# A planned attention and expert kernel: the negated maxima's transfers move from SyncE to ScalarE, with a new plan

## The chip, the cores and the metric

One core of a Trainium2 chip runs the kernel. The metric is the device time of one execution in microseconds, the median of several runs. PE is the tensor engine, DVE the vector engine, ACT the scalar engine (ScalarE), POOL GpSimd, SP the sync engine (SyncE), which here only issues transfers.

## What is computed

One pre-norm transformer layer in float32: causal attention with 16 heads of 16 columns, each row of the output scaled by a learned gate, then a mixture of experts (8 experts, 2 chosen for each token, and a shared one). B = 8 batches, S = 1024 tokens, E = 256 columns.

```python
Q, K, V = x @ Wq + bq, x @ Wk + bk, x @ Wv + bv        # x normalized, 16 heads
logits = jnp.einsum('bqhd,bkhd->bhqk', Q, K) * scale   # causal
attn = jax.nn.softmax(logits, axis=-1)
gate = jnp.tanh(g @ g_w2 + g_b2)[..., 0]               # g from a small network on x
x = x + einsum('bhqk,bkhd->bqhd', attn * gate, V) @ Wo + bo
...
h = silu(einsum('td,efd->tef', x, w1)) * einsum('td,efd->tef', x, w3)
x = x + einsum('tef,edf,te->td', h, w2, ew) + shared   # x normalized again
```

## The kernel before, in words

The work is cut into items: a kind of two letters and its place, as ("EX", n, g, s, p), batch n, group g of four heads, step s, pair p. `plan_work` lists all items with their engine, a cost in ns, a due time and the items that must come first; `Plan.run` then goes through a model of the five engines and picks for each engine, among the items that could start now, the one with the smallest due time. Two numbers bend this: `LATER` adds ns to the due time of a kind, and `SAME_TILING` is added to the due time of a PE item whose tiling of the array differs from the last one's, so the larger it is the longer PE stays with one tiling. What comes out is a fixed order for each engine; each engine's program is a walk through its order (`all_work`), with semaphore waits. An engine does its instructions strictly in that order.

Around the change, for each group and each half c of the 1024 queries:
- LD (SP, L969) loads stacked queries and keys to q_st and k_st. M (PE, L1912, and L1920 for the causal bars) makes the logits once with queries on the partitions, MR (DVE, L1548 and L1551) takes their row maxima to mx.
- MT (PE, L1932) turns the maxima, MN (ACT, L1344) writes them negated to rows_of (neg_max is a view of it), SM moves them: two transfers of 4 KB (L976) from rows_of to one row each of q_st, so that the scores come out with their maximum taken off.
- QK (PE, L1945) makes the scores with keys on the partitions. The first of each half waits for both transfers (semaphore nm_in). EX (ACT, L1362) takes the exponentials to probs, MK (POOL, L1179) masks the diagonal, PV (PE, L1965) sums them with the values, OE (ACT, L1371) copies the sums out and frees their bank.
- The tilings are rows for M and QK, columns for PV, full for everything else. Where the plan foresees that PE stands idle for 500 ns or more while sums are open, `keep_busy` puts up to eight filler matmuls there (L862), whose result adds zeros.

Beside these run the projections (L1882, L1896; DVE L1511 makes ql), the stores of queries and keys (SP L942, L943), the output projection (L1974), routing, and the experts (L2075, L2085, L2106; ACT L1423, L1438), with scatter and gather by POOL (L1211, L1223), the loads of routed rows xs<-xs_s (SP L1027) and, in the first batches, the clearing of their DRAM (SP L912, 512 KB each). SP issues every transfer but POOL's scatters and gathers, one after the other in its planned order. The plan charges SP ISSUE = 620 ns for each transfer.

Of the kernel before, what the change touches and what calls it, by code (L numbers as in the profile page):

```python
# [7 lines left out]
F32 = mybir.dt.float32  # L8
F32R = mybir.dt.float32r
ALU = mybir.AluOpType  # L10
ACT = mybir.ActivationFunctionType
# [9 lines left out]
PAIRS = GROUP // 2  # L21
# [3 lines left out]
GH = 16  # L25
# [14 lines left out]
QPC = CHUNK // P  # L40
# [59 lines left out]
ROWS_OF_HEAD = 64  # L100
# [8 lines left out]
FULL, ROWS, COLS = "full", "rows", "cols"  # L109
SWITCH, EXPOSED = 114, 104  # L110
PERIOD, KEEPS = 3413, 0.6
SAME_TILING = 14000
TAIL = {"PE": 155, "DVE": 88, "ACT": 112, "POOL": 45, "SP": 0}
HEARD = {"PE": {"PE": 0, "ACT": 37, "DVE": 37, "POOL": 75, "SP": 60}, "ACT": {"PE": 54, "ACT": 15, "DVE": 33, "POOL": 68, "SP": 60},
         "DVE": {"PE": 54, "ACT": 33, "DVE": 15, "POOL": 80, "SP": 60}, "POOL": {"PE": 54, "ACT": 33, "DVE": 33, "POOL": 40, "SP": 60},
# [1 line left out]
ISSUE = 620  # L117
# [60 lines left out]
def max_parts(u):  # L178
# [3 lines left out]
    for qt in qts:  # L182
# [4 lines left out]

LATER = {"AB": 8000, "AC": 15000, "AE": 22000, "AG": -1000, "AN": 4000, "AQ": -1000, "AR": -5000, "AS": -1000,  # L190
# [9 lines left out]


class Clock:
# [130 lines left out]
def plan_work():  # L333
    plan = Plan()
    add = plan.add
# [77 lines left out]
    def maxima(n, g):  # L413
        gi = n * GROUPS + g
        older = divmod(gi - 2, GROUPS)
        begin = at(n, g) - GROUP_T * 0.98
        for c in range(CHUNKS):
            m = g // (GROUPS // KE)
            add("SP", ("LD", n, g, c), 4 * ISSUE, begin - GROUP_T * (1.0 - 0.3 * c),
                [("PK", min(gi * CHUNKS + c + 1, K_HALVES - 1)), ("SQ", n, c, 2 * m), ("SQ", n, c, 2 * m + 1), ("QK",) + older + (LAST_STEP[c], SCORES[LAST_STEP[c]] - 1)],  # L420
                lands=9000 if n else 5000)
            units = [u for u in range(NMAX) if MAXU[u][0] == c]
            for u in units:
                _, p, kc, qts = MAXU[u]
                blocks = len(qts) * (1 if p is not None else PAIRS)
                due = begin + GROUP_T * 0.9 * u / NMAX
                add("PE", ("M", n, g, u), 240 if kc < c else 310 if blocks == 1 else 445, due,
                    [("BT",), ("LD", n, g, c), ("MT",) + older + (c,)], 2, ROWS)
                add("DVE", ("MR", n, g, u), sums(2 * sum(part[1] for part in max_parts(u)) * blocks // len(qts)) + 65 * len(qts), due + 1000, [("M", n, g, u)],
                    frees=(("M", n, g, u), None))  # L430
            due += 1500
            last = [("MR", n, g, units[-1])]
            if c:
                add("DVE", ("MJ", n, g), 95, due, last)
                last = [("MJ", n, g)]
            add("PE", ("MT", n, g, c), 60, due, last, 1, FULL)
            add("ACT", ("MN", n, g, c), 160, due, [("MT", n, g, c)] + ([("SM",) + divmod(gi - 1, GROUPS) + (c,)] if gi else []),
                frees=(("MT", n, g, c), None))
            add("SP", ("SM", n, g, c), 2 * ISSUE, due, [("MN", n, g, c)], lands=3600)

    def attention(n, g, s):
        c, kts, by_pair = STEPS[s]
# [192 lines left out]
def build(nc, ins, out):  # L635
# [4 lines left out]
    with ExitStack() as ctx:  # L640
# [161 lines left out]
        def q_half(n, g, c):  # L802
            return ((n * GROUPS + g) * CHUNKS + c) % Q_HALVES
# [79 lines left out]
        def _(sp):  # L883
# [84 lines left out]
                        to = q_st[r, q_half(n, g, c), :, :] if kind == 0 else k_st[r, k_half(n, g, c), :, :]  # L968
                        sp.dma_start(to.bitcast(F32), rows[j][:, :, cs]).then_inc(st_in[gi % 2][c], 16)  # L969

            def move_max(item, n, g, c):
                b, k = release["MN", n, g, c]
                sp.wait_ge(freed[b], k)
                for j in range(2):
                    to = q_st[ROWS_OF_HEAD * (j + 1) - 1:ROWS_OF_HEAD * (j + 1), q_half(n, g, c), :, :]
                    sp.dma_start(to.bitcast(F32), neg_max[j * PAIRS * QPC:(j + 1) * PAIRS * QPC, c, :].bitcast(F32)  # L976
                                 ).then_inc(nm_in[g % 2][c], 16)

            def store_o(item, n, g, c):
                b, k = release["OE", n, g, c]  # L980
                sp.wait_ge(freed[b], k)
# [70 lines left out]
            def load_ffn(item, i):  # L1052
                if i:
                    sp.wait_ge(wf_lo, i)
                sp.dma_start(wf_raw, ins["wf"][i]).then_inc(wf_in, 16)

            all_work(sp, "SP", {"AX": load_x, "WL": load_weights, "WC": load_constants, "BT": turn_bars, "XZ": clear_slots, "SQ": store_qk, "LD": load_stacks, "SM": move_max, "SO": store_o,
                                "CL": load_l, "CV": store_l, "CO": load_o, "SR": store_rest, "XL": load_slots,
                                "YS": store_slots, "RL": load_rest, "SY": store_y, "WF": load_ffn})
            for i in range(2):  # L1060
# [192 lines left out]
        def _(act):  # L1253
# [82 lines left out]
            def negate_max(item, n, g, c):  # L1336
# [3 lines left out]
                if gi:  # L1340
                    pn, pg = divmod(gi - 1, GROUPS)
                    if turn_of["QK", pn, pg, FIRST_STEP[c], 0] > turn_of["MT", n, g, c]:
                        act.wait_ge(nm_in[pg % 2][c], ((gi - 1) // 2 + 1) * 32)
                nc.scalar.activation(neg_max[:, c, :], bank(("MT", n, g, c))[0:GROUP * QPC, 0:P], ACT.Identity, scale=-1.0  # L1344
                                     ).then_inc(freed[release[item][0]], 1)

            def exponent(item, n, g, s, p):
                gs = (n * GROUPS + g) * NSTEP + s
                if first_wait("s_full", (n * GROUPS + g) * NSCORE + sum(SCORES[:s]) + p + 1):
                    act.wait_ge(s_full, (n * GROUPS + g) * NSCORE + sum(SCORES[:s]) + p + 1)  # L1350
                if p == 0 and gs >= 2:
                    of_group, older = divmod(gs - 2, NSTEP)
                    if turn_of["PV", of_group // GROUPS, of_group % GROUPS, older] > turn_of["QK", n, g, s, 0]:
                        if first_wait("pv_done", gs - 1):
                            act.wait_ge(pv_done, gs - 1)
                if SCORES[s] == PAIRS:
                    to, of = probs[:, s % 2, 2 * p:2 * p + 2, :], two_banks(("QK", n, g, s, p), CHUNK)
                else:
                    cols = CHUNK // PAIRS
                    to = probs[:, s % 2, :, 0:cols].rearrange("p (a j) c -> p j a c", j=2)  # L1360
                    of = two_banks(("QK", n, g, s, p), CHUNK).rearrange("p j (a c) -> p j a c", a=PAIRS)
                nc.scalar.activation(to, of, ACT.Exp, scale=DH ** -0.5).then_inc(freed[release[item][0]], 1)  # L1362
# [90 lines left out]
            def split_ffn(item, i):  # L1453
                if i == 0:
# [4 lines left out]
                nc.scalar.copy(hi, raw).then_inc(wf_hi, 1)  # L1459

            all_work(act, "ACT", {"AN": norm_x, "CM": mix_scale, "GC": gate_norm, "CN": norm_rest, "AC": copy_xt, "QH": queries_keys, "GE": gelu1, "GI": gelu2, "GL": gate_tanh,
                                  "MN": negate_max, "EX": exponent, "OE": copy_o, "CH": copy_hi, "XH": slots_hi,
                                  "CI": route_tanh, "RT": route_rows, "ET": expert_tanh, "HH": expert_high, "YC": copy_slots,
                                  "WH": split_ffn})

# [683 lines left out]
```

## Time and profile before

| | us |
|---|---|
| median of 3 runs | 1788.8 (1788.64 to 1791.04) |
| profiled execution, its time | 1798.91 |
| profiled execution, its span | 1797.1 |
| PE busy | 1650.4 (92%) |
| DVE, ACT, POOL busy | 1288.9, 1079.7, 810.5 |
| mean granted clock of PE | 0.968 |

Busy time is time in which an engine works on an instruction; issuing a transfer or waiting on a semaphore doesn't count. "SPq" is SP's queue issuing. "issue" in a chain or a wait is time in which nothing that the profile shows was waited for.

### The profile page before, as it was taken

Reading aid. Unit: us, or ns where it says so; the run is one execution under the profiler, and the core shown is the slowest. Engines: PE = TensorE matmul, PEld = TensorE weight load, DVE = VectorE, ACT = ScalarE, POOL = GpSimd, SP = SyncE. Lnnn points to the kernel's source line nnn. Section 1 sums busy time; section 2 is a strip of 40 time slices with the busy share of each in tenths; the row PEclk is TensorE's granted clock in tenths of the full one; section 3 lists DMA queues with packets and bytes.
Section 4 is the critical chain, followed back from the end, with each engine's and each line's share of the span. In section 5 each row is a group of like instructions: output and inputs, shape, how many; then the busy total and the mean of one; then the engine's idle time right before and its main releaser. Section 6 shows DMA issues by size and latency. Waiting matters only on the chain.

```text
span 1797.1 us, 34689 instructions
## 1 busy us (share of the span) xinstructions
PE 1650.4 (92%) x12770; PEld 979.4 (54%) x12770; DVE 1288.9 (72%) x2550; ACT 1079.7 (60%) x1808; POOL 810.5 (45%) x1390
## 2 busy tenths in 40 slices
PE   7799999889999999899998999999998989989889
PEld 3344455435544665456554566555654556657677
DVE  4777777857796768677696768877696656854666
ACT  3467755555657655675658666675557655657533
POOL 5325532453355221742238762543217674156761
PEclk9699999989999999999999999999999999999999
DMA  5557655544455444454455764534435655336440
GB/s 151 159 161 231 163 173 151 167 140 122 111 150 152 132 119 117 141 142 118 142 148 167 210 178 142 154 112 121 153 104 167 185 165 154 103 111 188 149 129 30
DMA packets 192709, 261.26 MB, mean 145 GB/s; under 512 B 19616, under 2 KB 127264, under 8 KB 192544
## 3 DMA queue, kind: packets, MB, share of 16 engines
q1 hardware_dynamic: 181792, 229.67, 44.3%
q0 software_dynamic: 10752, 29.37, 5.6%
q8 instruction: 105, 1.72, 0.4%
q14 instruction: 60, 0.49, 0.1%
HBM read 130.98 MB, written 127.40 MB: 144 GB/s over the span
## 4 chain that ended last, share of the span: by engine, by line
PE 53%; DVE 13%; ACT 10%; POOL 7%; DMA 7%; issue 5%; SPq 4%; another core or an unknown queue 1%; POOLq 0%; DVEq 0%; ACTq 0%
PE ps_all L2075 10%; PE ps_all L1965 10%; DVE mx L1551 6%; PE ps_all L1945 6%; PE ps_all L1912 6%; PE ps_all L2106 5%; ACT probs L1362 5%; PE ps_all L1896 4%; PE ps_all L1882 3%; PE ps_all L1974 2%; POOL xs_s L1211 2%; DMA qk_s<-ql 2%; PE ps_all L2085 1%; PE ps_all L1997 1%; DMA x<-in_x 1%
## 5 line engine op out<-in xcount | busy, mean ns | idle before, releaser
L1551 DVE TENSOR_REDUCE mx<-ps_all 128x2 f32<-128x1024 f32 (+2 forms) x640 | 620.6, 1005 | 157.1 <-PE ps_all L1912 84.2
L1362 ACT ACTIVATE probs<-ps_all 128x1024 f32<-128x1024 f32 x576 | 572.3, 1027 | 194.3 <-PE ps_all L1945 176.4
L1179 POOL TENSOR_SCALAR_AFFINE_SELECT probs<-probs 128x256 f32<-128x256 f32 (+1 forms) x448 | 190.8, 443 | 534.2 <-ACT probs L1362 529.9
L1965 PE MATMUL ps_all<-probs,vaug 128*32 128x512 f32 (+3 forms) x3072 | 323.0, 517 | 29.4 <-POOL probs L1179 18.9
L1912 PE MATMUL ps_all<-k_st,q_st 63*128 63x512 f32 (+3 forms) x1536 | 267.3, 399 | 41.0 <-ACT probs L1362 14.5
L1945 PE MATMUL ps_all<-q_st,k_st 64*128 64x512 f32 (+3 forms) x1536 | 262.3, 401 | 26.8 <-ACT probs L1362 11.8
L1912 PEld LDWEIGHTS ps_all<-k_st,q_st 63*128 63x128 f32 x1536 | 133.2, 190 | 162.7 <-issue 53.3
L1945 PEld LDWEIGHTS ps_all<-q_st,k_st 64*128 64x128 f32 x1536 | 128.9, 191 | 148.7 <-issue 65.6
L2075 PE MATMUL ps_all<-w_hi,x2h 128*128 128x512 f32 (+1 forms) x480 | 169.9, 354 | 3.2 <-DVE x2l L1600 2.2
L1808 DVE SCALAR_TENSOR_TENSOR act_t<-act_t,ps_all 128x256 f32<-128x256 f32 x168 | 70.2, 419 | 133.2 <-ACT act_t L1423 125.6
L1423 ACT ACTIVATE act_t<-ps_all 128x256 f32<-128x256 f32 x168 | 64.5, 385 | 161.3 <-PE ps_all L2075 116.4
L2075 PE MATMUL ps_all<-w_hi,x2l 128*128 128x512 f32 (+1 forms) x480 | 158.4, 330 | 0.0
L2075 PE MATMUL ps_all<-w_lo,x2h 128*128 128x512 f32 (+1 forms) x480 | 158.2, 330 | 0.0
L1965 PEld LDWEIGHTS ps_all<-probs,vaug 128*32 128x32 f32 x3072 | 72.3, 111 | 139.1 <-issue 96.9
L1211 POOL DMA_INDIRECT xs_s<-xnb,slot_u x112 | 111.9, 999 | 61.5 <-issue 41.3
L1223 POOL DMA_INDIRECT yab<-ys_s,slot_u x112 | 108.0, 964 | 33.0 <-issue 19.9
L2106 PE MATMUL ps_all<-w_hi,h_hi 128*128 128x256 f32 (+1 forms) x336 | 109.1, 325 | 4.8 <-DVE h_lo L1835 3.2
L2075 PEld LDWEIGHTS ps_all<-w_hi,x2h 128*128 128x128 f32 x480 | 92.4, 192 | 26.1 <-issue 17.6
L1438 ACT CAST h_hi<-ps_all 128x256 fp32r<-128x256 f32 x168 | 60.3, 374 | 63.9 <-PE ps_all L2085 57.0
L1882 PE MATMUL ps_all<-wvd,xt 128*128 128x384 f32 x256 | 96.3, 508 | 1.5 <-DVE ql L1511 0.9
L2075 PEld LDWEIGHTS ps_all<-w_hi,x2l 128*128 128x128 f32 x480 | 92.2, 192 | 8.6
L2075 PEld LDWEIGHTS ps_all<-w_lo,x2h 128*128 128x128 f32 x480 | 92.8, 193 | 5.6
(197 smaller groups left out, 2831.3 us busy)
## 6 DMA issues: line engine op xcount, KB each, us to landing
qk_s<-qh SPq DMA_DIRECT2D x116, 256.0 KB
q_st<-qk_s SPq DMA_DIRECT2D x128, 192.0 KB
k_st<-qk_s SPq DMA_DIRECT2D x128, 192.0 KB
xs<-xs_s SPq DMA_DIRECT2D x72, 256.0 KB
ys_s<-ysb SPq DMA_DIRECT2D x72, 256.0 KB
o_s<-o_sb SPq DMA_DIRECT2D x64, 256.0 KB
qk_s<-ql SPq DMA_DIRECT2D x57, 256.0 KB
xs_s<-ysb SPq DMA_DIRECT2D x20, 512.0 KB, 6.2
```

What stands on the lines that cost most here:

```text
L1179: last = nc.gpsimd.affine_select(out=block, in_=block, compare_op=ALU.is_ge, fill=0.0, base=0, pattern=[[0, heads], [1, P]], channel_multi ...
L1211: nc.gpsimd.indirect_dma_start(xs_s[i % 2], bass.IndirectOffsetOnAxis(ap=slot_u[:, n % 4, a, t:t + 1], axis=0), xnb[:, t, :], None).then_i ...
L1223: nc.gpsimd.indirect_dma_start(yab[:, t % 2, a, :], None, ys_s[SET_OF[n] % 2], bass.IndirectOffsetOnAxis(ap=slot_u[:, n % 4, a, t:t + 1], ...
L1362: nc.scalar.activation(to, of, ACT.Exp, scale=DH ** -0.5).then_inc(freed[release[item][0]], 1)
L1551: last = nc.vector.tensor_reduce(to[:, :, p, qt % QPC], both[:, :, at:at + keys], X_AXIS, ALU.max)
L1882: last = mm(bank(item)[:, 0:E + DP], xt[:, k, tt * P:(tt + 1) * P], wvd[:, k, :], start=(k == 0), stop=(k == KE - 1))
L1896: last = mm(bank(item), w[:, k, m * P:(m + 1) * P], xt[:, k, :], start=(k == 0), stop=(k == KE - 1))
L1912: last = mm(bank(item, j)[:, to:to + keys], q_st[r, q_half(n, g, c), p, qt % QPC * P:(qt % QPC + 1) * P], k_st[r, k_half(n, g, kc), p, 0:k ...
L1945: last = mm(bank(item, j)[:, to:to + cols], k_st[r, k_half(n, g, kt // QPC), a, kt % QPC * P:(kt % QPC + 1) * P], q_st[r, q_half(n, g, c), ...
L1965: last = mm(bank(first)[32 * h:32 * h + 32, q0 - c * CHUNK:], vaug[:, kt, g, h * VW:h * VW + 32], probs[:, s % 2, h, at:at + cols], start= ...
L2075: last = mm(bank(item)[:, to], x[:, buf, k, t * P:(t + 1) * P], w[:, k, cs], start=(k == 0 and j == 0), stop=(k == KE - 1 and j == 2))
L2106: last = mm(bank(first)[:, t * E:(t + 1) * E], h[:, z % 2, i * P:(i + 1) * P], w[:, cs], start=(item == first and i == 0 and j == 0), stop ...
```

## The change

SM becomes an item of ACT with a cost of 740 ns in the plan, and its two transfers are issued by ACT. `move_max` waits for the negation (which signals the semaphore of its bank) on ACT itself. SAME_TILING and the table LATER have other numbers.

```diff
-SAME_TILING = 14000
+SAME_TILING = 5000
...
-LATER = {"AB": 8000, "AC": 15000, "AE": 22000, "AG": -1000, "AN": 4000, "AQ": -1000, "AR": -5000, "AS": -1000,
...
+LATER = {"AB": 19000, "AC": 24000, "AE": 24000, "AG": 1000, "AN": 12000, "AQ": -1000, "AR": -15000, "AS": -9000,
...
-            add("SP", ("SM", n, g, c), 2 * ISSUE, due, [("MN", n, g, c)], lands=3600)
+            add("ACT", ("SM", n, g, c), 740, due, [("MN", n, g, c)], lands=3600)
...
-            def move_max(item, n, g, c):
-                b, k = release["MN", n, g, c]
-                sp.wait_ge(freed[b], k)
-                for j in range(2):
-                    to = q_st[ROWS_OF_HEAD * (j + 1) - 1:ROWS_OF_HEAD * (j + 1), q_half(n, g, c), :, :]
-                    sp.dma_start(to.bitcast(F32), neg_max[j * PAIRS * QPC:(j + 1) * PAIRS * QPC, c, :].bitcast(F32)
-                                 ).then_inc(nm_in[g % 2][c], 16)
...
+            def move_max(item, n, g, c):
+                b, k = release["MN", n, g, c]
+                act.wait_ge(freed[b], k)
+                for j in range(2):
+                    to = q_st[ROWS_OF_HEAD * (j + 1) - 1:ROWS_OF_HEAD * (j + 1), q_half(n, g, c), :, :]
+                    act.dma_start(to.bitcast(F32), neg_max[j * PAIRS * QPC:(j + 1) * PAIRS * QPC, c, :].bitcast(F32)
+                                  ).then_inc(nm_in[g % 2][c], 16)
```

In the changed kernel the lines up to the removed function stand 1 higher in number, those between it and the added one 7 lower, and those behind the added one 1 higher: the negation is L1337 there, the moved issues L1345, the exponentials L1363, the row matmuls L1913 and L1946, the sums L1966, the fillers L863.

SP's order near the start, batch 0, before (q_st<-rows_of is SM):

```order
L969 DMA q_st<-qk_s 48x2x512 x2
L969 DMA k_st<-qk_s 48x2x512 x2
L976 DMA q_st<-rows_of 1x8x128 x2
L969 DMA q_st<-qk_s 48x2x512 x2
L969 DMA k_st<-qk_s 48x2x512 x2
L942 DMA qk_s<-xs 8x16x512 x2
```

and ACT's order at the first maxima in the changed kernel (rows_of<-ps_all is the negation, probs<-ps_all an exponential):

```order
L1337 ACTIVATE rows_of<-ps_all 16x128
L1345 DMA q_st<-rows_of 1x8x128 x2
L1317 ACT_TABLE_LOAD
L1317 ACTIVATE vh<-vh 128x8x128
L1321 ACTIVATE gt<-gt 128x128
L1363 ACT_TABLE_LOAD
L1363 ACTIVATE probs<-ps_all 128x1024 x2
L1327 ACTIVATE gate<-drift,small 128x8
L1363 ACTIVATE probs<-ps_all 128x1024
L1337 ACTIVATE rows_of<-ps_all 16x128
L1345 DMA q_st<-rows_of 1x8x128 x2
```

SP's row L976 is gone from between the loads of stacks, and ACT has a row of two issues behind each of its 64 negations: directly behind it at 33, with other ACT work between at 31. Of the 33, 21 have an exponential or a copy of sums right behind them.

PE's order in batch 1, group 3, where the maxima of the next batch's first half are turned (L1932, then L1896 with wk), before:

```order
L1945 MATMUL ps_all<-q_st,k_st 128x512 x4
L862 MATMUL ps_all<-bars,scan 64x512 x3
L1932 MATMUL ps_all<-ident,mx 16x128
L862 MATMUL ps_all<-bars,scan 64x512 x8
L1896 MATMUL ps_all<-xt,wk 128x512 x2
L1965 MATMUL ps_all<-probs,vaug 32x256 x4
L1965 MATMUL ps_all<-probs,vaug 32x512 x4
L1945 MATMUL ps_all<-q_st,k_st 128x384 x2
```

and in the changed kernel:

```order
L1946 MATMUL ps_all<-q_st,k_st 128x512 x2
L1966 MATMUL ps_all<-probs,vaug 32x256 x4
L1946 MATMUL ps_all<-q_st,k_st 128x512 x2
L1946 MATMUL ps_all<-q_st,k_st 128x384 x2
L1946 MATMUL ps_all<-q_st,k_st 128x128 x2
L1946 MATMUL ps_all<-q_st,k_st 128x384 x2
L1946 MATMUL ps_all<-q_st,k_st 128x128 x2
L1933 MATMUL ps_all<-ident,mx 16x128
L1897 MATMUL ps_all<-xt,wk 128x512 x2
L1966 MATMUL ps_all<-probs,vaug 32x512 x4
L1946 MATMUL ps_all<-q_st,k_st 128x256 x4
```

The fillers around the turn are gone, four steps of scores stand ahead of it, and sums (L1966) come between scores, one row at a time. Over the whole order PE changes its tiling 1035 times before and 1132 times after, and has 120 fillers before and 71 after.

## Rows read from the trace of the kernel before

**Rows 1.** The page, its head, part 1 and the granted clock of part 2
```profile
span 1797.1 us, 34689 instructions
...
PE 1650.4 (92%) x12770; PEld 979.4 (54%) x12770; DVE 1288.9 (72%) x2550; ACT 1079.7 (60%) x1808; POOL 810.5 (45%) x1390
...
PEclk9699999989999999999999999999999999999999
```

**Rows 2.** The page, part 4, the chain that ended last, by engine
```profile
PE 53%; DVE 13%; ACT 10%; POOL 7%; DMA 7%; issue 5%; SPq 4%; another core or an unknown queue 1%; POOLq 0%; DVEq 0%; ACTq 0%
```

**Rows 3.** Windows: us, busy us of each engine, granted clock, DMA share, GB/s
```profile
0.00:300.00 300.00, 261.55 (x1911) 131.28 (x1912) 208.55 (x360) 175.12 (x262) 128.09 (x285) 0.93 0.60 172
...
600.00:900.00 300.00, 283.69 (x2255) 172.82 (x2251) 222.21 (x428) 181.57 (x305) 98.79 (x184) 0.99 0.46 129
```

**Rows 4.** The tile rows_of: durations min/median/max in ns
```profile
L976 SPq DMA_DIRECT2D q_st<-rows_of x128: 625/663/1994, 49.9 to 1611.5; - x128
L1344 ACT ACTIVATE rows_of<-ps_all x64: 247/262/269, 45.2 to 1610.5; 16x128 fp32r<-16x128 f32 x64
```

**Rows 5.** The chain in order of time, from 968 us: start, us, what
```profile
972.21 0.16 ACT rows_of L1344
972.37 0.02 issue
972.39 0.64 SPq L976
...
973.08 0.62 SPq L976
...
973.74 0.60 SPq L942
...
979.43 0.04 issue
979.47 6.83 DMA xs<-xs_s
```

**Rows 6.** Timeline of PE at 231.60: start, us, instruction, idle time before it
```profile
231.60 1.05 PE L1945 MATMUL ps_all<-q_st,k_st 64*128 64x512 f32 x4 [1.74 <-DMA q_st<-rows_of]
```

**Rows 7.** The chain in order of time, from 218 us
```profile
224.72 0.64 SPq L976
...
225.41 6.14 DMA q_st<-rows_of
...
231.60 1.05 PE ps_all L1945 x4
```

**Rows 8.** Who waited for whom, SP's queue: us in total, times, longest
```profile
SPq L976 <- ACT rows_of L1344: 72.6, 28, 8.4
```

**Rows 9.** Who waited for whom, all engines
```profile
POOL yab L1223 <- POOL rr L1236: 12.1, 36, 0.8
```

**Rows 10.** ACT's groups by line: busy, mean ns, idle before and its releasers
```profile
L1362 ACT ACTIVATE probs<-ps_all 128x1024 f32<-128x1024 f32 x576 | 572.3, 1027 | 194.3 <-PE ps_all L1945 176.4 <-issue 8.7 <-remote 6.5
```

**Rows 11.** Timeline of PE from 701 us, a change of tiling
```profile
701.08 0.28 PE L2106 MATMUL ps_all<-w_lo,h_hi 128*128 x1
...
701.20 0.28 PE L2106 MATMUL ps_all<-w_hi,h_lo 128*128 x1
...
701.41 0.50 PE L1912 MATMUL ps_all<-k_st,q_st 63*128 63x384 f32 x4
```

**Rows 12.** Timeline from 368 us: fillers, SP's long issues, PE's wait
```profile
370.26 1.91 PE L862 MATMUL ps_all<-bars,scan 128*64 128x512 bf16 x8
...
371.32 1.58 SPq L912 DMA_DIRECT2D xs_s<-ysb  x1
...
372.94 3.01 SPq L976 DMA_DIRECT2D q_st<-rows_of  x2
...
381.04 1.08 PE L1965 MATMUL ps_all<-probs,vaug 128*32 128x256 f32 x8 [6.96 <-POOL probs L1179]
...
385.86 3.37 PE L862 MATMUL ps_all<-bars,scan 128*64 128x512 bf16 x8
```

More of the change, by code:

```diff
@@ L1055, in load_ffn @@
                 sp.dma_start(wf_raw, ins["wf"][i]).then_inc(wf_in, 16)
-            all_work(sp, "SP", {"AX": load_x, "WL": load_weights, "WC": load_constants, "BT": turn_bars, "XZ": clear_slots, "SQ": store_qk, "LD": load_stacks, "SM": move_max, "SO": store_o,
+            all_work(sp, "SP", {"AX": load_x, "WL": load_weights, "WC": load_constants, "BT": turn_bars, "XZ": clear_slots, "SQ": store_qk, "LD": load_stacks, "SO": store_o,
                                 "CL": load_l, "CV": store_l, "CO": load_o, "SR": store_rest, "XL": load_slots,
@@ L1461, in _ @@
             all_work(act, "ACT", {"AN": norm_x, "CM": mix_scale, "GC": gate_norm, "CN": norm_rest, "AC": copy_xt, "QH": queries_keys, "GE": gelu1, "GI": gelu2, "GL": gate_tanh,
-                                  "MN": negate_max, "EX": exponent, "OE": copy_o, "CH": copy_hi, "XH": slots_hi,
+                                  "MN": negate_max, "SM": move_max, "EX": exponent, "OE": copy_o, "CH": copy_hi, "XH": slots_hi,
                                   "CI": route_tanh, "RT": route_rows, "ET": expert_tanh, "HH": expert_high, "YC": copy_slots,
```

19 rows, old and new, of the table LATER are left out of this document.

## The prediction

> **What bounds the kernel now.** I read the page's head first. The tensor engine is busy 92% of the span and holds 53% of the chain that ended last [rows 1, 2], so what changes the time is what makes PE wait or issue more. PE's idle time is 1797.1 − 1650.4 = 146.7 us, 8% of the span; ACT is busy 60% and holds 10% of the chain, DMA landings 7% and SP's own issuing 4%. The clock column and the windows say when PE ran slowly: 0.93 of full clock in the first 300 us, 0.99 from 600 to 900 [rows 1, 3].
>
> Then the transfers that the change moves. Each pair of SP issues at L976 follows one negation on ACT (L1344). The tile's view gives 128 issues of 663 ns in the median, 1994 ns at most, and 262 ns for a negation [rows 4]. In the chain SP starts 25 ns after the negation ends and is done with both 1.33 us later [rows 5]. By the timeline this is so in 31 of the 64 pairs; in the others SP is busy or waits for something queued ahead, up to 5.6 us. Who suffers from that? PE waited for these landings once, 1.74 us at 231.60 [rows 6], at the end of a piece of the chain in which the second transfer took 6.14 us from the start of its issue to its landing [rows 7]. The scores that need the maxima stand far behind them in PE's order. So the moved transfers are hidden nearly everywhere, and their latency is not what the kernel pays for.
>
> SP pays: it waited 72.6 us for the negations and spent some 128 × 0.66 = 85 us issuing [rows 4, 8], and everything behind stood in line. In the chain the load xs<-xs_s is issued at 979.47 at the end of an unbroken run of SP issues whose first two are L976's [rows 5].
>
> **What the change does, term by term.**
>
> *Removed from SP.* Ten L976 issues lie on the chain (counted over the whole chain in stretches of 300 us; three of the ten stand in [rows 5, 7]), 10 × 0.65 = 6.5 us, and the stall of 1.7 us at 231.60. I book **−8.2 us**. At least 0 (the next DMA in the line is late for its own reason), at most (72.6 + 85) × 11%, SP's and the DMAs' share of the chain, = −17 us [rows 2, 4, 8].
>
> *Added to ACT.* The same 128 issues. No row shows a DMA issued by ACT. The nearest rows are SP's: 1.33 to 1.38 us for a pair, so 64 × 1.38 = 88 us of ACT's queue. In the new order 33 pairs stand directly behind their negation, where ACT must let it finish; POOL's wait for its own predecessor before an issue is 12.1 / 36 = 0.34 us a time [rows 9], so 33 × 0.34 = 11 us more, 99 us in all. The lower end is 0: with a long ACTIVATE running (1027 ns each at L1362, [rows 10]) the sequencer may issue beneath it, as may be the case for the other 31. ACT sat idle 194.3 us before the exponentials alone, most of it for PE, so much of this is absorbed. I take ACT's share of the chain, 10%: 99 × 0.10 = **+9.9 us**, ends 0 and +50 (half of it exposed).
> The plan charges ACT 740 ns a pair; against SP's 1380 ns the planner would be short by 0.64 us at 64 places, 41 us that no shift has made room for.
>
> *More changes of tiling on PE.* SAME_TILING falls from 14000 to 5000. I counted the changes between L1912, L1920, L1945 (row tiles), L1965 (column tiles) and all others, leaving L862 out: 1035 before, 1132 after, 97 more. A following matmul of the same kind starts 0.12 us after the last one, the first of another tiling 0.21 us after it (701.08, 701.20, 701.41, [rows 11]): 97 × 0.09 = **+8.7 us**; between 0, where PE waits anyway, and 97 × 0.20 = +19.
>
> *Fewer fillers.* L862 holds PE busy where the planner foresees it waiting: 120 before, 71 after, as at the place shown in the order, where 8 of 8 go. Eight take 1.91 us at full clock [rows 12], 0.24 each: 49 × 0.24 = **−11.8 us**, since each stood for about that much foreseen idle time. Where the wait comes all the same the gain is 0, and more when the clock falls: after 6.96 us of idle PE the same eight take 3.37 us [rows 12]. Upper end +5.
>
> *The other shifts.* They move every engine's order and no row has their price. All they can do is shrink or grow PE's 146.7 us of idle time. The fillers fell by 41%; a tenth of that, 4%, is what I dare to carry over to the idle time outside them: **−6.0 us**, between −20 and +20.
>
> Sum: −8.2 + 9.9 + 8.7 − 11.8 − 6.0 = −7.4 us. The profiled execution took 1798.9 us, span 1797.1, some 10 us over the median of 1788.8; a difference is made against its rows and laid on the median: 1788.8 − 7.4 = **1781.4 us**.
>
> **A rule weighed.** SP goes from issue to issue in 0.04 us while a transfer takes over 6 us to land [rows 5], and one issue lasted three times the median [rows 4]. The Trainium skill, DMA: Bandwidth & Descriptors, section Issuing engines are not separate DMA queues, says that starting transfers from several engines saves only the time on the sequencer, usually small. By that the gain from freeing SP would be the 6.5 us at most, and landings would come no sooner; my −8.2 would be −6.5. The same skill, Perfetto Trace Analysis, section DMA Instruction — HWDGE, has an issuing sequencer lock the one descriptor generator; by it an ACT issue could wait for an SP issue. No row of before can show either on ACT.
>
> **Rivals.**
> *A: ACT is blocked and the kernel is slower, about 1805 us.* Mechanism: an exponential queued behind a pair of issues is 1.4 to 1.7 us late; its bank comes free late, the next scores wait, and the sums behind them. Place: the 33 pairs straight behind their negation, of which 21 in the order are followed at once by an exponential or by the copy that frees a bank, and the pairs issued in a crowded queue: SP's second pair at 372.94 took 3.01 us for both, beside the 512 KB clears of L912 and a POOL scatter, and PE then stood still for 6.96 us [rows 12]. Price: if 30 of the 99 us reach PE in place of 10, and the unplanned lateness undoes the term of the shifts (−6) and half of the fillers' (−5.9), the sum is −7.4 + 20 + 12 = +25; with half of these two, −7.4 + 16 = +9; the middle is +16.6, 1805 us. It decides from some 20 us of exposed ACT time on, a fifth. For it: EX waits are in the chain in all stretches and PE's idle before L1945 is mostly ended by ACT; against it: ACT has 40% idle time. With 17 us of ACT's 99 on the path the forecast is already a tie (−7.4 + 7).
> *B: nothing that can be told, about 1788 us.* The transfers were hidden anyway, ACT's issues are too, and 97 more tilings (+8.7) pay for the fillers (−11.8). For it: PE waited for these landings once. This is also what happens if the shifts only reshuffle.
> *C: more than forecast, about 1769 us.* SP's freed time is worth its upper end (−17), ACT issues beneath running ACTIVATEs (0 in place of +9.9): −7.4 − 8.8 − 9.9 = −26; the tilings may take up to 19 in place of 8.7, I give them 6 of that: −20.
>
> **How the numbers follow.** Chances: the forecast (1773 to 1785) 0.38, C 0.17, B 0.18, A 0.27. About 0.2% (3.6 us) can be told from no change here. So faster 0.56, same 0.18, slower 0.26. The range takes C's middle and most of A: 1764 to 1806 (left out: the far ends of both, 2 in 10); the forecast's own is 1773 to 1785.
>
> **What would show it.** Right: ACTq issues at the moved line of about 0.65 us, median, with ACT's busy time as before; SP's waits without the 72.6; PE busy near 1650 and its idle time 5 to 20 us shorter; L862 at 71. A shows as ACT waiting between the negation and the next ACTIVATE ("issue" or the queue's own time before L1363), more idle before L1946 ended by ACT, and a clock below 0.968. C shows as ACT's issues overlapping ACTIVATEs and the DMA share of the chain under 7%. B shows as equal idle time in all windows. The forecast is wrong if PE's idle time grows, or if it shrinks by over 20 us.

## The result, and the profile after

The changed kernel takes 1792.0 us (median of 22 runs, 1786.68 to 1803.46), the kernel before 1787.14 beside it (22 runs, 1774.64 to 1794.38): 0.37% slower, ratio 1.0037, 95% interval 1.0023 to 1.0051. That is 6.6 us more where 7.4 us less were forecast. Single executions lie up to 12 us from their median (before 1774.64, changed 1803.46), so a single profile can't show this difference: the profiled execution of the changed kernel spans 1790.3 us, less than the 1797.1 of before [rows 1], and only views that don't hang on the total can be compared.

The page of the changed kernel, part 1, its clock, its queues and its chain by engine:

```profile
span 1790.3 us, 34567 instructions
...
PE 1636.7 (91%) x12721; PEld 974.4 (54%) x12721; DVE 1298.4 (73%) x2550; ACT 1079.7 (60%) x1806; POOL 809.4 (45%) x1390
...
q10 hardware_dynamic: 2048, 0.53, 0.2%
...
PE 50%; DVE 15%; ACT 9%; POOL 7%; DMA 7%; issue 5%; SPq 3%; another core or an unknown queue 1%; ACTq 1%; DVEq 0%; POOLq 0%
```

PE works 14 us less than in [rows 1] and stands still for 1790.3 − 1636.7 = 153.6 us, 7 more than before. The 49 fillers less are the whole of the first figure: the trace's groups by line have 37.5 us of PE for the 120 fillers before and 23.7 for the 71 after. Half of it came back as idle time. A new queue, q10, carries the moved transfers. ACT's busy time is the same to 0.1 us, because issuing isn't counted as busy; the new cost hides in "ACTq 1%" of the chain.

The tile's view of the changed kernel (durations in ns, min/median/max), which answers to [rows 4]:

```profile
L1345 ACTq DMA_DIRECT2D q_st<-rows_of x128: 627/627/1534, 43.6 to 1603.7; - x128
```

ACT issues a transfer in 627 ns, SP in 663. The plan's 370 ns each was too little for the issue itself; SP's row was the right one to take. Two places of the timeline of ACT in the changed kernel (start, us, instruction, idle time before it) show what a pair does to ACT. A pair directly behind its negation:

```profile
69.95 0.25 ACT L1337 ACTIVATE rows_of<-ps_all 16x128 fp32r<-16x128 f32 x1
...
70.23 1.29 ACTq L1345 DMA_DIRECT2D q_st<-rows_of  x2
70.34 0.78 PE L1946 MATMUL ps_all<-q_st,k_st 64*128 64x384 f32 x4
...
71.56 1.02 ACT L1363 ACTIVATE probs<-ps_all 128x1024 f32<-128x1024 f32 x1 [1.36 <-PE ps_all L1946]
```

and one with other work between:

```profile
1178.21 0.25 ACT L1337 ACTIVATE rows_of<-ps_all 16x128 fp32r<-16x128 f32 x1
1178.36 0.36 ACT L1424 ACTIVATE act_t<-ps_all 128x256 f32<-128x256 f32 x1
1178.49 0.63 ACTq L1345 DMA_DIRECT2D q_st<-rows_of  x1
1178.63 1.00 ACT L1363 ACTIVATE probs<-ps_all 128x1024 f32<-128x1024 f32 x1
1179.15 0.63 ACTq L1345 DMA_DIRECT2D q_st<-rows_of  x1
```

In the first ACT computes nothing from 70.20 to 71.56. In the second it computes from 1178.21 to 1179.63, the issues beneath it, and is idle for 0.19 us until 1179.82, where the second issue has ended at 1179.78. So the pair costs by its place: ACT's queue issues beneath instructions that it has already handed on, and ACT stands idle for long only where the pair must first wait for the negation. Over the trace the time from the end of the last ACT instruction before a pair to the start of the next one after it is 1.45 us in the median at the 33 pairs directly behind, and 0.01 us at the other 31. The Trainium skill, Perfetto Trace Analysis, section DVE / Act Engine Instruction, says that the sequencer is free for the next instruction once it has pushed the last into the engine's wait queue; by that the second picture is what one should expect, and the trace agrees.

Not all of the 1.45 us is the pair's. With the same order and the pairs on SP (held_sp and held_sp_again below) ACT stands idle behind these same 33 negations for 39.2 and 41.4 us in all, 1.26 and 1.25 in the median, because what comes next waits for its own producer. In the changed kernel it is 55.7 us, and 54.4 in a second trace (after_again). The pairs add about 15 us to ACT's idle time there, not 33 × 1.45. Nor are the other 31 quite free: in the 2 us behind those negations ACT is idle for 21 us in all, and for 16 with the pairs on SP.

A small trap of the views: the first exponential's 1.36 us is put down to PE's scores. By PE's row they began at 70.34 and took 0.78 us, so they were there at 71.12, while ACT's second issue ran until 71.52. About 0.9 of the 1.36 us ACT would have waited in any case, and 0.4 are the issue's. The view puts the whole of it down to the semaphore.

SP's queue in the changed kernel, at the sums' copies (us in total, times, longest):

```profile
SPq L975 <- ACT o_sb L1372: 127.9, 42, 11.1
```

The 72.6 us that SP waited for the negations [rows 8] are gone from its queue, as foreseen, and its wait at the sums' copies is longer. L975 is L982 before:

```profile
SPq L982 <- ACT o_sb L1371: 42.4, 25, 7.1
```

Part of both differences is the new order's. With the same order and the pairs on SP, the two rows of held_sp are:

```profile
SPq L988 <- ACT o_sb L1377: 60.5, 27, 10.8
...
SPq L982 <- ACT rows_of L1350: 32.1, 18, 7.1
```

So the move itself took 32 us of waits off SP and added 67 at the sums' copies, where SP now arrives earlier and waits for the same producer.

### The profile page after: what moved, and what is told of

Read it like the earlier page. It is cut to its first block, busy times and chain, and to the rows that moved or that the text cites. A ratio compares the mean times of both kernels' runs of the same rounds, so it can differ in the third digit from the quotient of the medians.

```text
span 1790.3 us, 34567 instructions
## 1 busy us (share of the span) xinstructions
PE 1636.7 (91%) x12721; PEld 974.4 (54%) x12721; DVE 1298.4 (73%) x2550; ACT 1079.7 (60%) x1806; POOL 809.4 (45%) x1390
## 4 chain that ended last, share of the span: by engine, by line
PE 50%; DVE 15%; ACT 9%; POOL 7%; DMA 7%; issue 5%; SPq 3%; another core or an unknown queue 1%; ACTq 1%; DVEq 0%; POOLq 0%
PE ps_all L2076 9%; PE ps_all L1966 9%; PE ps_all L2107 6%; DVE mx L1552 6%; PE ps_all L1946 6%; PE ps_all L1913 6%; ACT probs L1363 5%; PE ps_all L1975 3%; PE ps_all L1897 3%; PE ps_all L1883 3%; POOL xs_s L1204 2%; DMA xa<-in_x 2%; PE ps_all L2086 2%; DMA qk_s<-ql 2%
## 5 line engine op out<-in xcount | busy, mean ns | idle before, releaser
L1363 ACT ACTIVATE probs<-ps_all 128x1024 f32<-128x1024 f32 x576 | 575.3, 1027 | 192.8 <-PE ps_all L1946 165.9
L1966 PE MATMUL ps_all<-probs,vaug 128*32 128x512 f32 (+3 forms) x3072 | 315.6, 505 | 24.2 <-POOL probs L1172 17.7
L1913 PE MATMUL ps_all<-k_st,q_st 63*128 63x512 f32 (+3 forms) x1536 | 269.6, 400 | 44.0 <-ACT probs L1363 20.5
L1946 PE MATMUL ps_all<-q_st,k_st 64*128 64x512 f32 (+3 forms) x1536 | 260.4, 396 | 28.5 <-ACT probs L1363 13.3
L1913 PEld LDWEIGHTS ps_all<-k_st,q_st 63*128 63x128 f32 x1536 | 133.2, 191 | 177.1 <-issue 70.5
L1946 PEld LDWEIGHTS ps_all<-q_st,k_st 64*128 64x128 f32 x1536 | 128.4, 188 | 146.0 <-issue 57.2
L1966 PEld LDWEIGHTS ps_all<-probs,vaug 128*32 128x32 f32 x3072 | 70.0, 110 | 130.0 <-issue 88.8
L1549 DVE TENSOR_REDUCE mx<-ps_all 128x4 f32<-128x1024 f32 x64 | 78.1, 1220 | 28.9 <-PE ps_all L1921 19.7
```

The costliest lines, as they stand in the source:

```text
L1549: last = nc.vector.tensor_reduce(to[:, :, :, qt % QPC], both.rearrange("p j (a k) -> p j a k", a=PAIRS), X_AXIS, ALU.max)
L1913: last = mm(bank(item, j)[:, to:to + keys], q_st[r, q_half(n, g, c), p, qt % QPC * P:(qt % QPC + 1) * P], k_st[r, k_half(n, g, kc), p, 0:k ...
L1946: last = mm(bank(item, j)[:, to:to + cols], k_st[r, k_half(n, g, kt // QPC), a, kt % QPC * P:(kt % QPC + 1) * P], q_st[r, q_half(n, g, c), ...
L1966: last = mm(bank(first)[32 * h:32 * h + 32, q0 - c * CHUNK:], vaug[:, kt, g, h * VW:h * VW + 32], probs[:, s % 2, h, at:at + cols], start= ...
```

## The experiments

Theory 1: ACT standing still behind the negation costs the time. Theory 2: the move is free and the new order costs it. "Order held" means that every engine's order is the named kernel's, instruction for instruction, and only the named items move. Ratios are to the kernel before on the same chip, with a 95% interval. Microseconds are the ratio less one, times the median of before there (1767 to 1785). Each batch of runs had a chip of its own: held_act_at_once, held_act_later, held_sp and four_issues the first; after_late, one_issue, tiling_14000 and held_sp_one the second; two_bounded, one_bounded, no_fillers and cost_1400 the third; after_again, two_bounded_again, held_sp_again and held_act_one_behind the fourth; the last two the fifth.

The last column is the mean granted clock of PE over the executions of the run, and of before beside it.

| run | edit | ratio | us against before | clock, run / before |
|---|---|---|---|---|
| held_act_at_once | order of before, pairs on ACT directly behind | 1.0231 (1.0198 to 1.0264) | +41 | 0.963 / 0.973 |
| held_act_later | the same, up to two ACT items later | 1.0033 (1.0007 to 1.0059) | +6 | 0.972 / 0.973 |
| held_act_one_behind | the same, one ACT item later | 1.0085 (1.0064 to 1.0106) | +15 | 0.971 / 0.975 |
| held_sp, held_sp_again | order of the changed kernel, pairs on SP | 0.9987 (0.9965 to 1.0008), 1.0007 (0.9990 to 1.0025) | −2, +1 | 0.969 / 0.973, 0.970 / 0.975 |
| after_again | the changed kernel | 1.0040 (1.0021 to 1.0060) | +7 | 0.970 / 0.975 |
| four_issues | changed kernel, four issues for two | 1.0309 (1.0276 to 1.0343) | +55 | 0.957 / 0.973 |
| one_issue, one_issue_again | changed kernel, one issue for two | 0.9982 (0.9962 to 1.0003), 0.9971 (0.9950 to 0.9992) | −3, −5 | 0.970 / 0.974, 0.970 / 0.974 |
| held_sp_one | held_sp with one issue for two | 0.9980 (0.9955 to 1.0005) | −4 | 0.970 / 0.974 |
| after_late | changed kernel, pairs two ACT items later | 1.0075 (1.0051 to 1.0099) | +13 | 0.969 / 0.974 |
| two_bounded, two_bounded_again | changed kernel, 28 of the 33 pairs one item later | 0.9961 (0.9939 to 0.9983), 1.0025 (1.0009 to 1.0041) | −7, +4 | 0.976 / 0.976, 0.969 / 0.975 |
| one_bounded, one_bounded_again | the same with one issue for two | 0.9921 (0.9892 to 0.9949), 0.9993 (0.9971 to 1.0015) | −14, −1 | 0.975 / 0.976, 0.968 / 0.974 |
| no_fillers | before without its 120 fillers | 1.0003 (0.9982 to 1.0024) | +1 | 0.968 / 0.976 |
| tiling_14000 | changed kernel, SAME_TILING 14000, planned anew | 1.0254 (1.0224 to 1.0283) | +45 | 0.958 / 0.974 |
| cost_1400 | changed kernel, pair charged 1400, planned anew | 1.0093 (1.0059 to 1.0128) | +16 | 0.967 / 0.976 |

The clock column has to be read with the times. Among the executions of before on one chip, a straight line through times and clocks gives 12 to 16 us less for 0.01 of clock more. All runs in the new order but two have 0.970 or less, also those with the pairs on SP, so a fall from 0.973 or more comes with the order alone. The two are two_bounded and one_bounded on the third chip. Whether a lower clock makes a run slow, or the idle time of a longer run lowers the clock, these columns alone don't tell.

### The move alone, the order alone

```diff
+    for item in [item for item in plan.order["SP"] if item[0] == "SM"]:
+        plan.order["SP"].remove(item)
+        plan.order["ACT"].insert(plan.order["ACT"].index(("MN",) + item[1:]) + 1 + 0, item)
```

> The order of before on every engine, but each pair of transfers issued by ACT directly behind its negation (64 of 64, against 33 of 64 in the changed kernel). ACT is blocked 64 x 1.4 = 90 us. Theory 1 (ACT's blocked queue costs the time): 10 to 20 us over before. Theory 2 (the new order costs the time, the move is free): within 4 us of before. SP's waits lose the 72.6 us in either.

> The order of before on every engine, the pairs issued by ACT up to two ACT items behind the negation (58 of 64 not directly behind it), so that they run beneath an ACTIVATE. Theory 1: 3 to 8 us over before, half or less of held_act_at_once. Theory 2: within 4 us of before.

> The order of the changed kernel on every engine, but the pairs given back to SP at their planned place (1132 tilings, 71 fillers). Theory 1: 5 to 10 us faster than before, since the new order pays once ACT is free. Theory 2: 5 to 9 us slower than before, as the changed kernel is.

held_act_at_once is 41 us slower, over twice what theory 1 gave it, and held_act_later 6. held_sp is within noise of before, so theory 2 falls: the new order, with its 97 more tilings and 49 fewer fillers, takes the same time as the old one. It does so at a clock lower by 0.004 to 0.005. At 12 to 16 us per 0.01 that is an estimated 5 to 8 us, which the order must gain elsewhere; what gains them was not looked into. Theory 1's own number for held_sp, 5 to 10 us faster, didn't come either.

The waits of PE on the exponentials in held_act_at_once (us in total, times, longest) show the way of the 41 us:

```profile
PE ps_all L1915 <- ACT probs L1365: 26.9, 46, 2.8
...
PE ps_all L1948 <- ACT probs L1365: 20.4, 34, 1.9
```

PE waits for the exponentials before the row matmuls for 26.9 + 20.4 = 47.3 us. The same two waits of before:

```profile
PE ps_all L1912 <- ACT probs L1362: 14.5, 33, 1.4
...
PE ps_all L1945 <- ACT probs L1362: 11.8, 23, 2.7
```

26.3 us: 21 more now. PE's idle time as a whole went from 146.7 to 1824.0 − 1654.9 = 169.1 us, 22 more. A late exponential frees its banks late, and the next scores or maxima stand behind them. The other 19 us don't show as idle time. The run's clock is 0.010 under that of before beside it, by the line above an estimated 12 to 16 us. The two traces don't show it, since the profiled execution of before has a low clock itself (0.968, against 0.965).

### The dose

```diff
                 for j in range(2):
+                    for a in range(PAIRS):
...
+                        act.dma_start(to.bitcast(F32), rows.bitcast(F32)).then_inc(nm_in[g % 2][c], 16)
```

> The changed kernel with each of the two transfers cut in two, four issues of some 0.63 us in place of two: ACT is blocked another 1.25 us 64 times, 80 us. Theory 1: another 10 to 20 us, 17 to 27 us over before. Theory 2: as the changed kernel, 5 to 10 us over before.

```diff
-                for j in range(2):
...
+                to = q_st[ROWS_OF_HEAD - 1:2 * ROWS_OF_HEAD:ROWS_OF_HEAD, q_half(n, g, c), :, :]
+                act.dma_start(to.bitcast(F32), neg_max[:, c, :].bitcast(F32)).then_inc(nm_in[g % 2][c], 16)
```

> The changed kernel, its order held, the two transfers made one that writes both rows of q_st: ACT is blocked 0.65 us less, 64 times. Theory 1: at the 33 places behind a negation 21 us less, half exposed, 10 us less than the changed kernel, so 1 to 6 us under before. Rival: one transfer of twice the size is issued in the same 1.3 us, and nothing changes (5 to 9 us over before).

The tile's view of four_issues, then its chain by engine:

```profile
L1347 ACTq DMA_DIRECT2D q_st<-rows_of x256: 580/581/2579, 44.1 to 1648.2; - x128
```

```profile
PE 50%; DVE 13%; ACT 11%; DMA 8%; POOL 5%; issue 5%; ACTq 5%; SPq 2%; another core or an unknown queue 1%; DVEq 0%; POOLq 0%
```

and the tile's view of one_issue:

```profile
L1344 ACTq DMA_DIRECT2D q_st<-rows_of x64: 503/518/1126, 43.9 to 1589.5; - x64
```

four_issues costs 48 us more than the changed kernel where theory 1 gave 10 to 20. All issues of four_issues together take 160.3 us of ACT's queue, those of the changed kernel 85.8, those of one_issue 33.9. Against before the three take +55, +7 and −3 or −5 us. So 75 us more cost 48 us (0.65 each), and 52 us less give back 10 to 12 (0.2 each): the first part of a pair is mostly hidden, and each part after it more and more on the path. What fits into a wait that is there anyway costs nothing. The clock of four_issues is 0.013 under after_again's, by the same estimate 16 to 21 of the 48 us; PE's busy time rose by 21 us (1636.7 to 1657.9) and its idle time by 25 (153.6 to 178.8). ACTq's share of the chain says the same: 5% of four_issues, 1% of the changed kernel, 0% of one_issue. One transfer for both rows costs 518 ns, less than one of the two that it replaces, so the rival, that a transfer of twice the size is issued in the same time as two, falls.

ACT's idle time tells more than the length of the issues. Summed over the 3 us behind each of the 64 negations, and set beside the same order with the pairs on SP:

| run | ACT idle there, us | more than with the pairs on SP | time against before, us |
|---|---|---|---|
| before | 71 | | |
| held_act_later | 80 | 8 | +6 |
| held_act_one_behind | 91 | 19 | +15 |
| held_act_at_once | 114 | 43 | +41 |
| held_sp, held_sp_again | 74, 77 | | −2, +1 |
| one_issue, one_issue_again | 78, 77 | 2 | −3, −5 |
| changed kernel, after_again | 90, 90 | 14 | +7, +7 |
| four_issues | 139 | 63 | +55 |
| two_bounded, two_bounded_again | 89, 90 | 14 | −7, +4 |
| after_late | 82 | 7 | +13 |

In the old order the time follows the added idle time of ACT nearly one for one, in the new order for the changed kernel about half and for four_issues most of it. That is theory 1, in its own currency. The 3 us cover the issues; by 5 us behind, ACT has caught up half of the 43 (22 left). Two rows don't fit: two_bounded (below), and after_late, which has another loss.

### The same place in the new order, and what SP's time is worth

> The changed kernel with each pair moved two ACT items behind its negation (0 of 64 directly behind it, against 33). Theory 1 (what costs is ACT standing still behind the negation, about half of it exposed, as held_act_at_once and four_issues showed): 4 to 9 us less than the changed kernel, so within 3 us of before. Rival (any issue on ACT costs, wherever it stands): as the changed kernel, 5 to 9 us over before.

after_late was to gain 4 to 9 us against the changed kernel and lost some 6. All 64 pairs stand away from their negation, but by a fixed count of items, however long these take: from the negation's end to the end of the second issue it is 2.6 us in the median and 19.1 us at most, against 1.3 and 6.8 in the changed kernel. A wait of PE in after_late (us in total, times, longest):

```profile
PE ps_all L1949 <- DMA q_st<-rows_of: 6.2, 3, 3.6
```

PE now waits for the landings, 6.2 us in the matmuls, where it never did in the changed kernel. What was a hidden latency was in part one no more. Whether these 6.2 us are the whole of the loss isn't shown.

> The changed kernel, its order held but for this: a pair directly behind its negation changes places with the one ACT item behind it, where that item was planned to start within 2.5 us (5 of 64 stay directly behind it, against 33). after_late moved every pair by two items and made some land 19 us late; here none moves by more than one. Theory 1 (ACT standing still behind the negation costs, and after_late lost by late landings): 4 to 9 us less than the changed kernel, within 3 us of before. Rival (an issue on ACT costs wherever it stands): as the changed kernel, 5 to 9 us over before.

> two_bounded with one transfer in place of two. Theory 1: one_issue gave 3 us under before with 33 places behind the negation; without them another 3 to 6 us, 6 to 9 us under before. Rival: as one_issue, 3 us under before.

These two gave the best times of all on their chip, where before itself took 1767 us, 15 to 20 us less than on the others. On another chip they didn't hold:

> two_bounded once more beside the changed kernel. Theory 1 (ACT standing still behind the negation costs): 8 to 15 us less than after_again, 3 to 10 us under before.

> one_bounded once more, since two_bounded did not hold on another chip (0.39% under before there, 0.25% over it here). If halving the issues is what counts: 3 to 10 us under before on any chip. If its 0.79% was that chip's: within 3 us of before.

two_bounded_again is 0.25% over before, 2 us under after_again beside it (1787.6 and 1789.5 us), within noise. So the place alone, one item later, gives nothing there that can be told, and the table above shows no less idle time of ACT than in the changed kernel: the pair now stands out behind the one item above it. Why the chips differ was not found, but the clock differs with the ratio: before has 0.976 and 0.975 on the two, two_bounded 0.976 on the first and 0.969 on the second, one_bounded 0.975 and, on the fifth chip, 0.968. one_issue, which held, has 0.970 both times.

> The changed kernel, word for word, beside the next three on one chip. 5 to 9 us over before (0.37% on record).

> The changed kernel's order with the pairs on SP once more. Theory 1: 5 to 10 us less than after_again. Against two_bounded_again it tells what taking the pairs off SP is worth once ACT issues them beneath its work: 0 if SP has room, 3 to 8 us more than two_bounded_again if SP's queue is worth something.

> The changed kernel with one transfer in place of two once more, beside one_bounded_again: 1 to 5 us under before, as it was. One place later (one_bounded_again) should take off 2 to 4 us more, what two_bounded_again took off the changed kernel.

On one chip: held_sp_again 1783.1 us, after_again 1789.5. This is the change's own price in an order that is otherwise the same, 6.4 us, with a 95% interval of some 2 to 10. The clock is the same 0.970 in both. PE's idle time in the traces agrees: 153.6 and 154.3 us with the pairs on ACT (the changed kernel and after_again), 148.8 and 141.2 on SP (held_sp and held_sp_again), though two traces of one kernel can lie that far apart. one_issue_again is under before with its whole interval, and one_bounded_again is not better than it, so the halved issue is what pays, not the place.

> The order of before, the pairs issued by ACT one item behind the negation (6 of 64 directly behind it), the same rule as two_bounded. If the rule of place is all that counts: 3 to 8 us under before, as two_bounded. If the new order is needed (it was planned with time for the issues on ACT): within 4 us of before or up to 6 us over it, as held_act_later.

By the same rule of place the old order is 15 us slower than before, the new one 4 us slower or 7 us faster: the new order, planned with 740 ns on ACT for each pair, has more room for them (14 us of added idle time of ACT against 19). One item later came out worse than up to two (held_act_later, +6 us), on another chip. The traces show a likely reason: from the end of the last ACT instruction before a pair to the start of the next, ACT is idle for 0.84 us in the median of the 58 moved places in held_act_one_behind, and not at all in held_act_later. One such place, where the 0.56 us cast above the pair ended at 607.56 and the second issue at 608.46:

```profile
608.50 1.02 ACT L1367 ACTIVATE probs<-ps_all 128x1024 f32<-128x1024 f32 x1 [0.94 <-issue]
```

One short instruction doesn't cover 1.3 us of issues.

> held_sp (the changed kernel's order, the transfers at their planned place on SP) with one transfer in place of two: SP's queue has 64 issues of 0.66 us fewer, 42 us. If SP's time is worth the share of the chain that I gave it (11%): 5 us less, 5 to 9 us under before. Rival (SP has room): as held_sp, 0 to 5 us under before.

Beside it one transfer replaces two on SP. Taking 50 us of issues from SP's queue (88.2 to 38.1 us over the trace) moved the time from 0.9987 and 1.0007 to 0.9980, nothing that can be told. SP has room. On the same chip one_issue, with the same single transfer on ACT, takes 1778.4 us and held_sp_one 1777.5: once the pair is one transfer, it makes no difference which of the two engines issues it.

### Fillers, tilings and the planner's numbers

> The kernel before without its 120 filler matmuls (they add zeros), its order held otherwise. If a filler is 0.24 us of PE time on the path, as my term had it: 10 to 25 us less than before. If they stand in idle time: no change within 4 us, or slower by up to 20 us where the clock falls in their place.

```diff
-            if open_sums and plan.idle[item] >= IDLE_FROM:
+            if False and open_sums and plan.idle[item] >= IDLE_FROM:
```

Without the 120 fillers the kernel takes the same time on this chip (the third), but at a clock of 0.968 beside 0.976. At 12 to 16 us per 0.01 that is an estimated 10 to 13 us lost, so the fillers' own time, 37.5 us of PE in the trace of before, can't all stand in waits that cost nothing. The zero looks like two effects that cancel. No run holds the clock fixed, so this stays an estimate.

> The changed kernel with SAME_TILING back at 14000, planned anew (1014 tilings and 100 fillers in place of 1132 and 71). If the extra tilings cost 0.09 us each and nothing else counts: 118 x 0.09 = 11 us less than the changed kernel, 3 to 6 us under before. If the shifts fit only the order that they were made for, it is as slow or slower than the changed kernel: 7 to 20 us over before.

> The changed kernel with the pair charged 1400 ns in the plan, planned anew (1126 tilings, 72 fillers, 40 of 64 pairs directly behind the negation). If the wrong charge of 740 ns is what makes the move cost: 4 to 9 us less than the changed kernel. If the shifts fit only the order that they were made for: slower than the changed kernel, 10 to 40 us over before, as tiling_14000 was.

The rank is the reverse of the first expectation: with 118 changes of tiling fewer the kernel is some 39 us slower than the changed one. tiling_14000's span is 1835.3 us at a clock of 0.954, and its engines:

```profile
PE 1662.5 (91%) x12750; PEld 985.3 (54%) x12750; DVE 1296.6 (71%) x2550; ACT 1076.9 (59%) x1806; POOL 812.4 (44%) x1390
```

PE idles 1835.3 − 1662.5 = 172.8 us, 19 more than in the changed kernel, and its clock is 0.954 where that has 0.969. PE's busy time is 26 us longer, with 29 more fillers in it. Telling the planner nearly the true cost of a pair (cost_1400) is 0.93% slower than before, too, so the rival that the wrong charge is what costs finds no support. Both are planned anew with shifts that were made for other numbers. So neither tells the price of a tiling or of the wrong charge by itself; what they tell is that this plan answers to one changed number with 10 to 40 us, and that two plans may only be compared as orders held, not as settings.

## Why the prediction was wrong

The result of 1792.0 us lies in the range, the direction is the other one: the forecast of faster (0.56) failed and rival A's direction (0.26) came true, at two fifths of A's price (6.6 of 16.6 us). Two steps failed. The new order was booked with −9.1 us (fillers −11.8, shifts −6.0, tilings +8.7) and measured −2 and +1; SP's freed time was booked with −8.2 and gave nothing that a run could tell. These misses are 8.6 and 8.2 us, against 14 between forecast and result; ACT's +9.9 was some 3 too much the other way. Point by point:

- **Added to ACT, +9.9 us: near by number, not by reasoning.** With the order held the move as a whole costs 6.4 us, and if SP's side gave nothing, that is ACT's price. A pair takes 1.29 us (1.38 taken), and it does run beneath ACTIVATEs at the 31 places. But the sum laid 99 us of issues on ACT and took 10%, ACT's share of the chain, an average over all of ACT's work. In the traces the pairs add some 14 us of idle time to ACT, since it waits at many of these places anyway, and nearly half of that reaches the time. Two errors cancel here, and that is luck. Where no room was planned the share is far from 10%: 41 us for 86 us of issues (held_act_at_once), 48 us for another 75 (four_issues), about half to two thirds.
- **Removed from SP, −8.2 us: failed.** The pieces of the chain went, but not the time: SP now waits for producers that are late for their own reason, the lower end that I had named (0). With the order held it waits 67 us longer for the sums' copies (60.5 to 127.9), and held_sp_one, which takes 50 of the moved issues' 88 us off SP, gained nothing that can be told. The rule weighed in the prediction (the Trainium skill, DMA: Bandwidth & Descriptors, Issuing engines are not separate DMA queues: only the sequencer's time is saved) spoke for a smaller gain, and was nearer than my sum.
- **Fewer fillers, −11.8 us: failed.** Taking out all 120 moved the time by +0.03% and the clock from 0.976 to 0.968. The prediction had named a falling clock as an upper end (+5) and booked nothing for it. In the changed kernel PE's busy time did fall by 14 us, and its idle time grew by 7.
- **More tilings, +8.7, and the other shifts, −6.0: their sum with the fillers failed.** I had −9.1 us for the order as a whole; held_sp and held_sp_again measured −2 and +1 us. The shifts' −6.0 rested on a tenth of the fillers' fall, which no row bore out. What a tiling or a shift costs for itself stays open: no run changed only that.
- **B's argument, that the moved transfers were hidden anyway, held** for the landings: PE waited for none of them in the changed kernel. after_late shows the limit: with the pairs 1.3 us later in the median, and up to 19 us behind the negation, PE waited for three of them.
- The sum by measured terms: order −0.5 (mean of −2 and +1), move +6.4, together +5.9 us, against 6.6 measured. This is no independent test: the same runs of after_again and held_sp_again stand in it, and it says mainly that the result came again on another chip.

What the profile of the changed kernel was to show: ACTq issues near 0.65 us and SP without the 72.6, right; idle time of PE 5 to 20 us shorter, wrong, it grew by 7. Rival A's signs were to be more idle before the moved scores ended by ACT and a clock below 0.968: the first is there in small (below). The clock is not under 0.968 by the letter (0.969 in the profile, 0.968 over the 22 executions), but the 0.968 of [rows 1] is itself low for before, which has 0.973 to 0.976 on the five chips of the experiments. Beside before's 0.975 after_again has 0.970. That fall is no sign of A, since held_sp_again has the same 0.970. The waits of PE in the changed kernel, 33.8 us where before has 26.3 (32.1 in after_again, 30.1 in held_sp and 21.0 in held_sp_again, so one trace is uncertain by some 9 us):

```profile
PE ps_all L1913 <- ACT probs L1363: 20.5, 25, 6.9
...
PE ps_all L1946 <- ACT probs L1363: 13.3, 25, 1.2
```

## What to carry to other kernels

An engine's share of the chain doesn't price a new stall on it: ask which instruction stands right behind the new one and what frees what there, and how long the engine waits at that place anyway; what sticks out of that wait counts, and half of it to nearly all reached the time here, where it delayed the work that feeds the bound engine. In this kernel an issue on ACT was nearly free beneath a long instruction already handed on (some 5 us in all at 31 places), and a pair directly behind ACT's own last result left ACT idle for 1.45 us, where in this order it was idle for 1.25 us without the pair too; before moving issues, see whether two transfers can be one (518 ns for 1254 here; one_issue is the fastest that held on two chips, 0.18% and 0.29% under before, the first not clear of zero, and some 0.6% under the changed kernel; on SP the same single transfer did as well, 0.20% under before). Look at the clock beside the time: a change that takes work out can lower it and gain nothing, as no_fillers did. Compare orders held fixed: a planner that is run again answers with more than the edit under test.

## What the runs showed that I had not expected

- One transfer with both rows is issued faster (518 ns) than one of the two halves (627 ns), and a quarter costs nearly as much as a half (581 ns, four_issues).
- The plan's sensitivity: 14000 for 5000 in one number made 39 us, with a tenth fewer changes of tiling and a mean clock of 0.958.
- The same kernels against the same kernel before moved by 0.6% (two_bounded) and 0.7% (one_bounded) between two chips, outside their intervals, while one_issue moved by 0.1%. An interval of one chip is no interval for all.
